# Two-block transformer kernel on one core: where the shared up projections, the token gathers and the last groups' loads stand

## What is computed

```
x = L0_attn_x
xn = _layernorm(x, axis=-1)
x = x + _L0_attn_ref(xn, ...) + _L0_ffn_ref(xn, ...)
# attention: 128 heads; per head the 32 largest and 32 smallest keys with their values,
# softmax over q*key, choice by the sign of q, projection Wo
# feed-forward: softmax gate, 6 of 64 experts a token, capacity 128, shared expert of width 352
h = silu(einsum('ecd,eid->eci', xe, w1)) * einsum('ecd,eid->eci', xe, w3)
ye = einsum('eci,edi->ecd', h, w2)
z = silu(xf @ sw1.T) * (xf @ sw3.T) @ sw2.T
return (routed + z).reshape(Bb, Tt, D)
```

## Time and profile before

| | us |
|---|---|
| median of 3 runs | 614.75 |
| lowest, highest | 605.39, 618.04 |
| the profiled execution | 613.87 |
| its span on the core | 612.1 |
| busy in the span: PE, VectorE, ScalarE, GpSimd | 465.3, 381.4, 187.7, 237.6 |

### The profile page before, as it was taken

The page is one execution under the profiler, slowest core; times in us unless marked ns, Lnnn a source line. Parts: engine busy times, 40 slices in busy tenths (PEclk is TensorE's granted clock), DMA queues, the critical chain, the costliest instruction groups (busy, mean ns, idle before and its releaser), DMA issues.

```text
span 612.1 us, 9668 instructions
## 1 busy us (share of the span) xinstructions
PE 465.3 (76%) x2928; PEld 302.7 (49%) x2928; DVE 381.4 (62%) x1067; ACT 187.7 (31%) x479; POOL 237.6 (39%) x210
## 2 busy tenths in 40 slices
PE   4922999888777898778688978536889988657766
PEld 2611555455445554545455545213634777545645
DVE  4897687844553655455536556425769868577984
ACT  2651322223332333233333332211265303021122
POOL 3153466556555555555455542000002053022444
PEclk9965999979988977899789887857889999798898
DMA  8921498879878787877787874440000277566502
GB/s 313 341 84 43 109 297 186 206 176 238 211 197 203 173 196 201 212 184 197 197 201 167 211 163 84 120 172 14 2 0 1 52 182 104 112 121 126 129 7 70
DMA packets 63422, 91.80 MB, mean 150 GB/s; under 512 B 21120, under 2 KB 42464, under 8 KB 63264
## 3 DMA queue, kind: packets, MB, share of 16 engines
q1 hardware_dynamic: 50496, 70.19, 42.0%
q0 software_dynamic: 12896, 21.24, 17.6%
HBM read 72.89 MB, written 18.51 MB: 149 GB/s over the span
## 4 chain that ended last, share of the span: by engine, by line
PE 28%; DMA 28%; DVE 14%; SPq 11%; issue 9%; POOL 5%; ACT 4%; DVEq 0%; ACTq 0%; POOLq 0%
PE ps L1418 20%; DMA big<-kr_dram 9%; DMA big<-k_img 8%; DMA big<-tok_tab,big 7%; SPq L485 6%; POOL routed L624 2%; DMA big<-idx_dram 2%; PE ps L1423 2%; DVE big L1096 2%; PE ps L1521 2%; SPq L567 2%; DVE big L1011 1%; POOL big L617 1%; DVE big L1009 1%; DVE big L1396 1%
## 5 line engine op out<-in xcount | busy, mean ns | idle before, releaser
L1418 PE MATMUL ps<-big 128*128 128x352 f32 (+4 forms) x768 | 241.9, 459 | 9.2 <-DVE big L1074 6.2
L1418 PEld LDWEIGHTS ps<-big 128*128 128x128 f32 (+2 forms) x768 | 149.9, 208 | 71.4 <-issue 29.9
L624 POOL DMA_INDIRECT routed<-big x64 | 101.9, 1592 | 130.4 <-ACT big L792 114.4
L617 POOL DMA_INDIRECT big<-tok_tab,big x64 | 63.3, 990 | 31.2 <-issue 30.9
L1074 DVE COPY big<-ps 88x256 f32<-88x256 f32 x64 | 26.7, 417 | 66.3 <-PE ps L1506 64.3
L1066 DVE SCALAR_TENSOR_TENSOR big<-big,ps 128x176 f32<-128x176 f32 x64 | 21.6, 337 | 65.6 <-ACT big L787 65.5
L1423 PE MATMUL ps<-cst,big 128*128 128x128 f32 x144 | 32.5, 311 | 36.9 <-DMA big<-tok_tab,big 34.2
L782 ACT ACTIVATE big<-ps 128x256 f32<-128x256 f32 x64 | 24.6, 384 | 107.3 <-PE ps L1423 107.2
L1418 PE MATMUL ps<-xnT,big 128*128 128x512 f32 (+1 forms) x104 | 50.1, 623 | 0.9 <-ACT xnT L723 0.9
L787 ACT ACTIVATE big<-ps 128x176 f32<-128x176 f32 x64 | 20.3, 318 | 96.5 <-PE ps L1418 96.5
L805 ACT ACTIVATE big<-ps 128x512 f32<-128x512 f32 x64 | 34.7, 595 | 45.9 <-PE ps L1521 45.7
(11 more groups left out here) (187 smaller groups left out, 668.0 us busy)
## 6 DMA issues: line engine op xcount, KB each, us to landing
big<-in_w SPq DMA_DIRECT2D x64, 352.0 KB
big<-in_w SPq DMA_DIRECT2D x64, 176.0 KB
big<-q_dram SPq DMA_DIRECT2D x64, 72.0 KB
big<-kr_dram SPq DMA_DIRECT2D x24, 192.0 KB
big<-kr_dram SPq DMA_DIRECT2D x72, 64.0 KB
big<-idx_dram SPq DMA_DIRECT2D x16, 256.0 KB, 7.4
kr_dram<-big SPq DMA_DIRECT2D x12, 256.0 KB, 4.5
routed<-big POOLq DMA_DIRECT2D x2, 1152.0 KB, 16.0
```

The costliest lines, as they stand in the source:

```text
L617: nc.gpsimd.indirect_dma_start(xe[:, e % SLOTS, :], None, tok_tab, bass.IndirectOffsetOnAxis(ap=sidx[:, e:e + 1], axis=0))\
L624: nc.gpsimd.indirect_dma_start(routed[e % 2], bass.IndirectOffsetOnAxis(ap=sidx[:, e:e + 1], axis=0), ye[:, e % 2, :], None, compute_op=AL ...
L1418: last = nc.tensor.matmul(o, w, m, start=(n == 0), stop=(n == len(pairs) - 1))
```

## The change

1. **Shared up projections.** All six pairs move from the experts to the start of the program. `shared_up(0)` and `(1)` stand on TensorE ahead of the slot-key transposes, two more between the two halves of the v products, two behind them. ScalarE applies Silu to the one factor and copies the other (`shared_out`); GpSimd multiplies them (`shared_hidden`). The load of their weights goes ahead of two others. Nothing of the tanh form and VectorE's products is left.
2. **Token rows.** ScalarE copies the expert's gate column to its own tile right after `tokens_in`; a gather waits for that copy (`s_xefree`), and stands one place further ahead: e + 5 before `routed_add(e)`.
3. **Loads of groups.** In SyncE's loop `q_and_keys` goes behind the first expert's weights, `positions` behind the second's. Groups 13 and 15 get a second buffer for q, k and positions; block 1's weights go to the end of that list.
4. **VectorE's order.** Selection rounds are cut into single instructions around `hidden`; in the quads the one-hots and placed values stand elsewhere; the ternary steps, before in the groups behind the loop too, are all done in 8 of the quads (two a quad).
5. **Groups 12 to 15.** `values(n + 1)` goes on TensorE behind `x1_product`, and ScalarE's `values_out` behind `oT_copy`.

Tables that ScalarE loads by the program's list: before, one at the start and one ahead of the Sqrt of block 1. Now also one ahead of the first Silu, and one at the head of the quads' loop, between its first branch and the first Exp.

The last positions now stand ahead of block 1's weights. The diff, cut to its core:

```diff
+        sc_buf_at = sr_at - NT * (E + 2)
+        skgs = [skg, carve(4 * P // 2, ROWS, at=sc_buf_at).bitcast(BF16)]
+        qxs = [qx, v3(carve(4 * S // 2, ROWS, at=sc_buf_at + 256).bitcast(BF16), 4, S)]
...
+        idxbs = [idxb, carve(SETS * P // 2, at=sc_buf_at + 1280).bitcast(BF16)]
...
             sp.dma_start(wv, w_v).then_inc(s_wv, 16)
+            sp.dma_start(wsh13, w_sh13).then_inc(s_wsh, 16)
             sp.dma_start(w_fc1, w_fc).then_inc(s_wff, 16)
             sp.dma_start(w_pj1, w_pj).then_inc(s_wff, 16)
-            sp.dma_start(wsh13, w_sh13).then_inc(s_wsh, 16)
...
                 next_weights(3, u, only(3))
             for u in range(SLOTS):
                 next_weights(4, u, only(4))
-                if u == 2:
+                if u == 1:
                     sp.wait_ge(s_hot, 4)
                     positions(only(1))
+                if u == 2:
                     store_keys(1)
             sp.wait_ge(s_kst[1], 80)
+            sp.wait_ge(s_abs, 2)
+            second = IN_LOOP + 1
             with sp.Fori(1, IN_LOOP) as n:
                 for u in range(SLOTS):
                     next_weights(n + LAG, u, bass.ds(n + LAG, 1))
-                    if u == 1:
+                    if u == 0:
                         sp.wait_ge(s_lp, n * 4)
                         q_and_keys(bass.ds(n, 1))
-                    if u == 2:
+                    if u == 1:
                         sp.wait_ge(s_hot, n * 4 + 4)
                         positions(bass.ds(n + 1, 1))
-            for n in range(IN_LOOP, NG):
-                sp.wait_ge(s_lp, 4 * n)
-                q_and_keys(only(n))
-                if n == NG - 2:
-                    for i in range(2):
-                        sp.wait_ge(s_sc[i], 16 * (1 + E // 2))
-                        for b in range(B):
-                            sp.dma_start(racc[i][:, b * TPB:(b + 1) * TPB, :],
-                                         routed[i][b * S:(b + 1) * S, :].rearrange("(t p) d -> p t d", p=P))\
-                              .then_inc(s_racc[i][b], 16)
-                    sp.wait_ge(s_y, E + 1)
-                    sp.dma_start(w5, w_rkvgo).then_inc(s_w5, 16)
-                if n + 1 < NG:
-                    sp.wait_ge(s_hot, 4 * n + 4)
-                    positions(only(n + 1))
+            q_and_keys(only(second), qxs[1], skgs[1], s_qxl2)
+            positions(only(second), idxbs[1], s_idx2)
+            sp.wait_ge(s_lp, 4 * IN_LOOP)
+            q_and_keys(only(IN_LOOP))
+            sp.wait_ge(s_hot, 4 * IN_LOOP + 4)
+            positions(only(IN_LOOP + 2))
+            sp.wait_ge(s_lp, 4 * IN_LOOP + 4)
+            q_and_keys(only(IN_LOOP + 2))
+            for i in range(2):
+                sp.wait_ge(s_sc[i], 16 * (1 + E // 2))
+                for b in range(B):
+                    sp.dma_start(racc[i][:, b * TPB:(b + 1) * TPB, :],
+                                 routed[i][b * S:(b + 1) * S, :].rearrange("(t p) d -> p t d", p=P))\
+                      .then_inc(s_racc[i][b], 16)
+            sp.wait_ge(s_lp, 4 * IN_LOOP + 8)
+            q_and_keys(only(IN_LOOP + 3), qxs[1], skgs[1], s_qxl2)
+            sp.wait_ge(s_hot, 4 * IN_LOOP + 8)
+            positions(only(IN_LOOP + 3), idxbs[1], s_idx2)
+            sp.wait_ge(s_y, E + 1)
+            sp.dma_start(w5, w_rkvgo).then_inc(s_w5, 16)
+
...
             def token_gather(e):
                 if e >= SLOTS:
-                    pool.wait_ge(s_y, e - SLOTS + 2)
+                    pool.wait_ge(s_xefree, e - SLOTS + 1)
                 nc.gpsimd.indirect_dma_start(xe[:, e % SLOTS, :], None, tok_tab,
...
+            def shared_hidden(i):
+                rows = SROWS[i // B]
+                h = hs[0:rows, i // B, (i % B) * S:(i % B + 1) * S]
+                pool.wait_ge(s_sht, i + 1)
+                nc.gpsimd.tensor_tensor(h, h, sha[0:rows, i % 2, :], ALU.mult).then_inc(s_hs, 1)
+                pool.wait_ge(s_hs, i + 1)
+
+            for i in range(2):
+                shared_hidden(i)
+            for i in range(2, 4):
+                shared_hidden(i)
             v_rest(0)
             pool.wait_ge(s_vr, 1)
+            for i in range(4, NPAIR):
+                shared_hidden(i)
             v_rest(1)
             pool.wait_ge(s_vr, 2)
             pool.wait_ge(s_qp0, 1)
...
+            token_gather(SLOTS)
             for e in range(E):
+                if e + SLOTS + 1 < E:
+                    token_gather(e + SLOTS + 1)
                 routed_add(e)
-                if e + SLOTS < E:
...
+            def shared_out(i):
+
+                rows, bank = SROWS[i // B], (4, 2)[i % 2]
+                act.wait_ge(s_shp, 2 * i + 1)
+                nc.scalar.activation(hs[0:rows, i // B, (i % B) * S:(i % B + 1) * S], PS[bank][0:rows, :], ACT.Silu)
+                act.wait_ge(s_shp, 2 * i + 2)
+                if i >= 2:
+                    act.wait_ge(s_hs, i - 1)
+                nc.scalar.activation(sha[0:rows, i % 2, :], PS[bank + 1][0:rows, :], ACT.Copy).then_inc(s_sht, 1)
+
+            for i in range(2):
+                shared_out(i)
             act.wait_ge(s_skTp, 1)
             nc.scalar.activation(slotk, PS[6][:, :], ACT.Copy).then_inc(s_skT, 1)
+            v_copies(range(TPB))
+            for i in range(2, 4):
+                shared_out(i)
             v_copies(range(TPB, NT))
+            for i in range(4, NPAIR):
+                shared_out(i)
             v_second(0)
             for b in range(B):
                 act.wait_ge(s_qp, b + 1)
...
-            def tokens_in(e, u):
+            def tokens_in(e, u, group):
+
                 act.wait_ge(s_xeTp, e + 1)
                 nc.scalar.activation(xeT[:, u % 2, :, :], PS[0][:, 0:D].rearrange("p (c n) -> p c n", c=DC),
                                      ACT.Copy).then_inc(s_xeT, 1)
+                nc.scalar.activation(gate[:, u:u + 1], gates[:, u, u, group], ACT.Copy).then_inc(s_xefree, 1)
 
...
-            def scale_out(e, u, free, gate):
+            def scale_out(e, u, free):
                 act.wait_ge(s_yp, e + 1)
                 act.wait_ge(s_sc[u % 2], free)
-                nc.scalar.activation(ye[:, u % 2, :], PS[3][:, 0:D], ACT.Copy, scale=gate).then_inc(s_y, 1)
-
-            def shared_tanh(i):
-                rows = SROWS[i // B]
-                act.wait_ge(s_shp, 2 * i + 1)
...
             for n in range(IN_LOOP, NG):
                 exps(n, range(4))
-                if n + 1 < NG:
-                    values_out(n + 1)
                 if n == IN_LOOP:
                     act.wait_ge(s_qst, 64)
                 oT_copy(n - IN_LOOP)
+                if n + 1 < NG:
+                    values_out(n + 1)
...
-            def quad(n, done=None, last=False):
+            def quad(n, done=None, blocks=None, last=False):
+
 
                 for u in range(SLOTS):
                     e = n * SLOTS + (LAG * SLOTS + u)
                     hidden_T(e, u)
+                    if u == 0:
+                        place_values(n)
+                        one_hot(n + 1, 0)
+                    if u == 1:
+                        one_hot(n + 1, 3)
+                        if done:
+                            normalise(*done, slice(0, 5))
                     if u == 2:
                         out_copy(n)
+                    if blocks and u == 3:
+                        ternary(0, *blocks)
                     if not last or u + 1 < SLOTS:
                         hidden(e + 1, u + 1)
                     if u == 0:
-                        place_values(n)
-                    if u < 2:
-                        one_hot(n + 1, 2 * u)
-                        one_hot(n + 1, 2 * u + 1)
-                    if done and u == 0:
-                        normalise(*done, slice(0, 5))
+                        one_hot(n + 1, 1)
+                        one_hot(n + 1, 2)
                     if done and u == 1:
                         normalise(*done, slice(5, NORM))
-                    if done and u == 3:
-                        ternary(*done)
+                    if blocks and u == 2:
+                        ternary(1, blocks[0] - 1, blocks[1])
 
             quad(0)
             with dve.Fori(0, 8) as k:
-                quad(k + 1, (0, k, bass.ds(k, 1)))
+                quad(k + 1, (0, k, bass.ds(k, 1)), (k * 2 + 1, bass.ds(k, 1)))
             with dve.Fori(0, 2) as k:
                 quad(k + 9, (1, k + 8, bass.ds(k, 1)))
             quad(11, (1, 10, slice(2, 3)), last=True)
@@ -1208,14 +1266,12 @@
                 place_values(n)
                 if n + 1 < NG:
                     for k in range(4):
-                        one_hot(n + 1, k)
+                        one_hot(n + 1, k, (n + 1 - IN_LOOP) % 2 == 1)
                 k = n - 9
                 normalise(1, n - 1, slice(k, k + 1), slice(0, NORM))
                 out_copy(n)
-                ternary(1, n - 1, slice(k, k + 1))
                 x1_add(n - IN_LOOP)
```

(32 more changed lines are left out.)

147 lines of the change are left out of this document (74 added, 73 removed).

## The result

The changed kernel takes 577.74 us (median of 4 runs, 572.74 to 579.98), against 612.75 (4 runs) for the kernel before: ratio 0.949, 95% interval 0.936 to 0.962. The prediction said 565, within 546 to 592, and faster. Its direction and range hold; the median is 12.7 us above the forecast. The profiled execution took 579.98 us, span 578.2. Executions of one kernel differ by up to 3.4%, and the ratios here compare only those within 1.5% of their kernel's fastest.

The account below looks back on a forecast made before the run. It took TensorE to bound experts 1 to 15 and waits to pace the quads. From 613.9 us: start +10.3, experts -41.9, tables +2, groups -17.9, last ternary block -1.5, giving 564.9, say 565, within 546 to 592.

Parts of the forecast that it names:

- Start: Start of the program: shared products lengthen TensorE's list, first gather 11.8 us later, expert 0 ends 10.3 us later.
- taken back: Start: expert 0 no longer has a shared product (1.8 us) in front of it, so 1.5 us is deducted.
- the two waits: Experts: waits for k before a quad's logits and for token rows both go; experts take 264 us against 305.9.
- I expect about 60 of it in the first stage: Experts 1 to 15: about 60 us of the experts' 264, with 17.0 a quad.
- SyncE's longer row of issues: Quads: this or the weights hold each quad at 19.7 us, kernel at 596; chance 0.07.
- the scatter-adds: Expert pairs: landings stretched past 7.9 us set the pace; 580 at 8.4 us, 631 at 10; chance 0.03.
- With the pause goes most of the low clock: Experts: without the pause before the logits, TensorE mostly leaves 1.2 GHz; quads' mean clock over 0.95, from 0.89.
- in every quad: Quads: waits on landed adds or `expert_weights` in each one were listed as a sign of a wrong forecast.
- Groups: Groups 12 to 15: three intervals of 9.1 us, 27.3 against 45.2, so 17.9 us less; bounds 22.6 and 34.
- Transfers at 212 GB/s as the capacity: Experts: transfers are already the bound, so they take 287 us and the kernel 588; chance 0.14.
- Waits replaced one for one: Quads: other waits take over at 19.7 us each, only first stage and groups gain, kernel at 596; chance 0.07.
- Table loads bare: Head of the quads' loop: 11 exposed loads cost 14 us instead of 2, kernel at 577; chance 0.06.

Follow-up runs that it names:

- e4: Changed kernel without the shared expert's up projections, Silu, copies and products (zeros in their place): 562.38 us.
- e7: Changed kernel with slot transposes ahead of the q transposes, the absolute-sum product behind, and the first four gathers ahead of GpSimd's q work: 565.02 us.
- e2: Changed kernel with only GpSimd's order put back, gather e + 4 behind routed_add(e): 600.38 us.
- e3: Changed kernel with q_and_keys and positions back behind the second and third expert's weights in SyncE's loop: 600.26 us.
- e6: Changed kernel reloading only 16 of w2's 512 columns per expert (output differs): 554.57 us.
- e1: Changed kernel with Tanh in place of Silu, so the two added table loads go (output differs): 580.97 us.
- e9: Changed kernel with groups 12 to 15 loaded into one buffer again, last positions still ahead of block 1's weights: 582.83 us.
- e12: Changed kernel with SyncE's group transfers in experts 0 to 15 spread, one to three between two experts' weights: 572.12 us.
- e5: Changed kernel with four ye buffers and four scatter tables, only two read back: 575.47 us.

## Why the prediction came out as it did

**The sum.** It read 613.9 + 10.3 - 41.9 + 2 - 17.9 - 1.5. Measured are 15.2 for the start, -35.0 for the experts, nothing for tables, -17.4 for the groups, -1.9 for the end, and 2.0 and 3.3 in two places that had no term (ahead of group 12; block 1 at a lower clock). The sum starts from the profiled execution, 613.9, and by the profiled execution after, 579.98, it is 15.1 us short, not 12.7. Every large term has its sign and mechanism; the error is one of sizes.

**Start: right place, 5 us too small.** TensorE's list ends last, as said; e4 confirms the products as the cause (10.2 us) and e7 the order (7.1 at the first gather, 5.1 at expert 0). The first gather came at 68.9 for the 66.0 forecast, and these 3 us are about what the gate products took more, 6.93 us for 3.68 before, ahead of any edit. The other 2 are the 1.5 us "taken back": from first gather to expert 0 it took 13.4 us and not less than the 12.9 of before. Why the shared product gone from there gave nothing back is open; TensorE's clock in that stretch was 0.54, before 0.64.

**Experts: the two waits.** Right that both set the quad, and that they go. The quads took 204.3, forecast 12 x 17.0; with 203.0 to 209.3 for the same code, so close a hit is partly luck. e2 and e3 show that each removal is necessary and that their worths don't add.

**The largest miss: "I expect about 60 of it in the first stage."** That stage took 66.5 (62.6 to 63.6 in three runs of the same code), 6.5 of the 6.9 us by which the experts' term is off. The 60 doesn't follow from the rate that the sum used: at 230 GB/s the 14.7 MB of the first stage give 64 us and the 46.1 MB of the quads 200. It asks for 245, the rate of the best quad before. Measured are 222 and 226 GB/s, 225 over both. In the first stage other things hold next to the bytes (e6, with fewer of them, is no quicker there): weights issued behind rows of group transfers, and landed adds. Both were in the prediction, as rivals: "SyncE's longer row of issues" and the scatter-adds. I gave these to the quads, and the scatter-adds as the slower case.

Also wrong for this stage is "With the pause goes most of the low clock". It held in the quads (0.97 for 0.89). In the first stage the clock fell to 0.82, and TensorE was busy 55.4 us where 43.6 were forecast. The same eight products of an up projection, ahead of the first wait for weights and right behind it:

```profile
82.52 2.29 PE L1474 MATMUL ps<-big 128*128 128x352 f32 x8 [0.35 <-ACT big L831]
...
102.38 4.42 PE L1474 MATMUL ps<-big 128*128 128x352 f32 x8 [3.54 <-DMA big<-in_w]
```

The granted clock was 1.00 in the first and 0.50, 1.2 GHz, in the second, after 3.5 us without work. So a wait here costs more than its own length. How the 6.5 us divide among weights, landed adds and this clock was not separated.

In the quads the landed adds stayed near the limit that the prediction worked out, 7.9 us: three are on the chain there, of 7.7, 7.6 and 9.4 us. In the first stage five are, of 7.0 to 8.1. The longest of each, first stage first:

```profile
116.74 8.06 DMA routed<-big
```
```profile
265.09 9.42 DMA routed<-big
```

Waits on landed adds "in every quad" were to be a sign of being wrong. They came in eight of the twelve, 18.1 us of ScalarE's waiting in all, of which four tables give back nothing measurable (203.8 for 204.3). So the sign came largely true without what it stood for.

**Tables: 2 us.** Nothing measurable (e1).

**Groups: right to 0.5 us.** The sum came closer than its parts: the three intervals took 9.6, 7.3 and 10.9 us, forecast 9.1 each, and in the last VectorE waited 5.26 for positions. Of the argument e9 shows a third, the buffers. **Rivals.** Transfers at 212 GB/s as the capacity: wrong, the stages run at 222 and 226, e12's at 248. Waits replaced one for one: wrong in the quads, and nearly true of a kernel with only one of the two edits (medians of 600 in e2 and e3; the rival said 596). Table loads bare: wrong (e1), and that its 577 is the median measured is an accident.

## What to carry to other kernels

Where two waits pace a loop, price the removal of both together: with one of them the quads here gained 4.7 of 32.2 us in the traces, and an experiment that undoes one shows nearly the whole. When work moves ahead of an in-order engine's chain, look for what small step stands at that chain's end behind a wait of its own: here two 128 x 128 transposes behind a product on absolute sums cost 7 us at the first gather and 5 at the first expert, and moving them ahead gave a kernel quicker than both. Before an edit is carried to another kernel, read in that kernel's trace whether the wait is there: the spreading of SyncE's transfers met 6.3 us of waits for weights in one kernel and 1.2 in the other. A mean transfer rate is no forecast for a stage in which a queue's order holds the next load back.

## What was not expected of the hardware

TensorE's gate products, the same code ahead of any edit, took 3.68 us before and 3.82 in e7, but 6.92 to 6.93 in the changed kernel and in all the other experiments. In before, in e7 and in the changed kernel the engine stood idle until 8.7 to 8.9 us and then did the same 16 transposes, and the DMA engines moved some 415 GB/s beside the gate products. The granted clock reads 1.00 in the first 20 us of all three, so no row shows a lower one. The cause stays open; it is worth some 3 us of every time here, and e7's start has them in its favour.

Scatter-adds landed after 5.6 us at the median before, 8.4 at most; after, those on the chain, which are the late ones, took 7.0 to 9.4 us. Weights issued behind a row of group transfers landed 10.9 us after their issue in e5.
